# TensorE's order within a slot: the two score tiles ahead of the second transposed chunk, and where the values' products stand

## The reference

```python
x = x + attn_a(layernorm(x), Wq, bq, Wk, bk, Wv, bv, Wo, bo)   # causal mask
x = x + ffn(layernorm(x), g_info, W_qkv, W_proj, b_proj)       # tokens in two classes; a token sees its class and 5 registers
x = x + attn_b(layernorm(x), Wqkv, Wo)                         # rotary embedding, full attention
x = x + ffn(layernorm(x), g_info, W_qkv, W_proj, b_proj)

scores = einsum('bhqd,bhkd->bhqk', Qh, Kh) / sqrt(16)
attn = softmax(scores + mask)
out = einsum('bhqk,bhkd->bhqd', attn, Vh) @ Wo + bo
```

## Time and profile before

| | |
|---|---|
| median of 3 runs | 5044.56 us (5038.67 to 5048.72) |
| the profiled execution | 5051.34 us, span 5049.7 us |
| PE busy | 4459.8 us, 88% of the span |
| DVE, ACT, POOL busy | 64%, 50%, 33% |
| mean granted TensorE clock | 0.965 of full speed |
| stage 0, causal: first to last slot | 1344.4 us, PE busy 1186.9, clock 0.97 |
| stage 1, split | 1337.1 us, PE busy 1166.2, clock 0.94 |
| stage 2, rotary | 1246.5 us, PE busy 1124.9, clock 0.98 |
| stage 3, split | 986.2 us, PE busy 936.7, clock 0.99 |

### The profile page before, as it was taken

One profiled execution on the slowest core, in us unless ns is written; L12 is line 12 of the kernel. 1 busy time (PEld: TensorE's weight loads), 2 busy tenths in 40 slices (PEclk: granted clock), 3 DMA queues, 4 the chain that ended last, 5 costly groups with the idle time before them and its releaser, 6 DMA issues. The chain is left out here.

```text
span 5049.7 us, 70670 instructions
## 1 busy us (share of the span) xinstructions
PE 4459.8 (88%) x26116; PEld 1880.7 (37%) x26116; DVE 3220.1 (64%) x6578; ACT 2547.4 (50%) x3362; POOL 1655.6 (33%) x922
## 2 busy tenths in 40 slices
PE   4899999999869988999886899999999589999999
PEld 2454545455413333333332233333333223333333
DVE  4555555455447677777772766776676277777776
ACT  1444444444425555555453465556555356656555
POOL 2354554545422425344355033333333400000000
PEclk8999999999979999999998899999999889999999
DMA  5353544444323243342432342343344223333331
GB/s 152 99 153 125 148 129 145 133 132 139 97 69 102 83 112 97 94 119 87 113 93 77 83 117 93 105 122 105 95 120 118 66 71 86 86 86 91 89 91 42
DMA packets 302269, 525.23 MB, mean 104 GB/s; under 512 B 58340, under 2 KB 236136, under 8 KB 285544
## 3 DMA queue, kind: packets, MB, share of 16 engines
q1 hardware_dynamic: 259432, 485.06, 33.5%
q10 hardware_dynamic: 42496, 35.66, 2.2%
HBM read 316.97 MB, written 201.46 MB: 103 GB/s over the span
## 5 line engine op out<-in xcount | busy, mean ns | idle before, releaser
L887 DVE TENSOR_REDUCE neg_max<-scores 128x1 f32<-128x512 f32 (+3 forms) x4096 | 2486.6, 636 | 1279.1 <-PE scores L1246 746.4
L1105 ACT ACTIVATE probs<-scores_t 128x1024 f32<-128x1024 f32 (+2 forms) x2048 | 1925.7, 946 | 1571.0 <-PE scores_t L1279 1091.1
L1246 PE MATMUL scores<-k_stack,q_stack 98*128 98x512 bf16 (+4 forms) x4096 | 1435.5, 373 | 285.1 <-DVE neg_max L887 197.8
L1279 PE MATMUL scores_t<-q_stack,k_stack 100*128 100x512 bf16 (+3 forms) x4096 | 1189.3, 364 | 67.7 <-DMA q_stack<-shift_rows 66.4
L1246 PEld LDWEIGHTS scores<-k_stack,q_stack 96*128 96x128 bf16 (+1 forms) x4096 | 397.1, 97 | 1688.0 <-DVE neg_max L887 1240.2
L1300 PE MATMUL o_ps<-probs,values 128*32 128x512 f32 (+1 forms) x8192 | 1019.7, 570 | 0.3 <-ACT probs L1105 0.3
L1279 PEld LDWEIGHTS scores_t<-q_stack,k_stack 100*128 100x128 bf16 x4096 | 377.9, 99 | 389.3 <-issue 142.3
L730 POOL TENSOR_TENSOR parts<-qk_f,parts 128x1024 bf16<-128x1024 f32 x128 | 272.5, 2129 | 678.6 <-ACT parts L1148 519.5
L750 POOL TENSOR_TENSOR sim_inv<-sim_parts,minus_half 128x64 f32<-128x64 f32 x32 | 337.6, 10550 | 206.0 <-DVE sim_parts L970 206.0
L743 POOL TENSOR_TENSOR x_res<-x_res,o_bias_s 128x1024 f32<-128x1024 f32 x32 | 75.5, 2359 | 987.5 <-DMA x_res<-x_after 987.5
L701 POOL TENSOR_SCALAR var_eps<-mean_var 128x4 f32<-128x4 f32 x64 | 14.6, 229 | 1084.5 <-DVE mean_var L851 1084.5
(11 more groups left out here) (118 smaller groups left out, 4045.4 us busy)
## 6 DMA issues: line engine op xcount, KB each, us to landing
q_stack<-q_parts SPq DMA_DIRECT2D x1536, 64.0 KB, 2.7
values<-v_stage SPq DMA_DIRECT2D x64, 1024.0 KB, 4.2
values<-values SPq DMA_DIRECT2D x64, 1024.0 KB, 6.2
k_parts<-parts SPq DMA_DIRECT2D x192, 256.0 KB, 2.7
q_parts<-parts SPq DMA_DIRECT2D x192, 256.0 KB, 4.3
k_stack<-k_parts SPq DMA_DIRECT2D x256, 192.0 KB, 3.2
k_stack<-k_parts SPq DMA_DIRECT2D x256, 128.0 KB, 3.2
x_after<-x_res ACTq DMA_DIRECT2D x48, 512.0 KB, 2.9
```

The costliest lines, as they stand in the source:

```text
L887: nc.vector.tensor_reduce(neg_max[:, h % G, t:t + 1], bank[:, 0:n], AX.X, ALU.max, negate=True).then_inc(max_done.sem, 1)
L1105: nc.scalar.activation(probs[c][:, h % G, 0:n], st[i][:, 0:n], ACT.Exp).then_inc(exp_done.sem, 1)
L1246: last = nc.tensor.matmul(bank[:, 0:n], q[0:r, h, t * P:(t + 1) * P], k[0:r, h, 0:n], start=True, stop=kind != CAUSAL)
L1279: last = nc.tensor.matmul(st[i][:, off:off + L - q0], k[0:ROWS, h, kt * P:(kt + 1) * P], q[0:ROWS, h, q0:L], start=True, stop=kind != CAUSAL)
```

## The change

On PE, m0 and m1 move behind chunk 1, and the values' products move up in front of m2. A slot is now: chunk 0, turns of place 0, chunk 1, m0, m1, values' products, m2, (the extra tile of a split stage's slot 1), m3, turns of place 1. On DVE the list follows: all four maxima stand in the slot's second half, behind whatever belongs to place 0. The semaphores' counts, the tables of turns, buffers, ACT's, POOL's and SP's lists are as before.

```diff
@@ vector block, body @@
                     for place in range(2):
-                        if m:
-                            maximum(B + m[0], m[1], 2 * place)
+                        if place and m:
+                            for t in range(T - 1):
+                                maximum(B + m[0], m[1], t)
                         if place and kind == SPLIT and slot == EXTRA_AT:
                             extra_max(B)
-                        if m:
-                            maximum(B + m[0], m[1], 2 * place + 1)
+                        if place and m:
+                            maximum(B + m[0], m[1], 3)
@@ tensor block, body @@
                     scores_t(B, h0, c, 0)
+                    turns(0)
+                    scores_t(B, h1, c, 1)
                     max_tile(0)
                     max_tile(1)
-                    turns(0)
-                    scores_t(B, h1, c, 1)
+                    if B.n + off >= 0:
+                        output_sums(B + off, g, kt)
                     max_tile(2)
                     if kind == SPLIT and slot == EXTRA_AT:
                         extra_tile(B)
-                    if B.n + off >= 0:
-                        output_sums(B + off, g, kt)
                     max_tile(3)
                     turns(1)
```

## The result

The changed kernel takes 5215.35 us (median of 4 runs, 5210.34 to 5216.99) against 5046.64 us for the kernel before on the same chip: a ratio of 1.0332, 95% interval 1.0312 to 1.0352. It is 3.3% slower; the prediction said 5240 us, 3.9% slower.

A forecast was written before the change was run, and what follows sets the result against it. PE sets the pace, with place-0 turns timed by the turn bank's read and turnless slots by a ring through DVE. Costs of 283 us less gains of 88 give +195, so 5240 us, 3.9% slower; range 5100 to 5340.

The forecast's parts named there:

- item 5: Stage 1's slot 2, behind the long packing of maxima: m3 comes 1.6 us earlier, a gain of 26 us.
- Item 1: Turns of place 0 other than `og`, 21 of 36: m0 and m1 fall onto the path, costing 122 us.
- item 2: `og` turns in place 0 after `sh`, 15 of 36: DVE's shift-row copy comes later too, costing 134 us.
- item 3: In slots at PE's own pace, m3 waits 0.07 us for the maximum of m1, costing 27 us.
- Item 4: Slots without turns stay at 3.11 us against 3.12; only the first behind a turn gains, 19 us in all.
- the ring: In slots without turns, a cycle of waits through DVE times the slot: 3.12 us before, 3.11 after.
- The rival by which a new order saves nothing at two full banks: At the tiles' two banks, a skill's rule on too few PSUM buffers: Item 4 gives 0 instead of 19 us.
- The statistics and the normalisation: Work delaying the maxima of slots 7 to 9: nothing booked, as DVE's list there is as long as before.
- The same: Lost covers and regained waits balance, PE regaining 197.8 us and half of item 2 not coming: 5045 us, chance 0.05.
- Faster: All 192 packings in stages 0 to 2 halt PE, each giving 1.6 us: 4959 us, chance 0.09.
- Much slower: The later shift DMA meets the next batch's loads in two more groups per batch: 128 us more, 5370 us, chance 0.13.
- The check in the waits: In the table of waits, PE's waits for the turn bank, released by ACT and DVE, grow by some 200 us.

The follow-up runs named there:

- the run with that slot alone: Kernel before, with the values' products ahead of m2 in stage 1's slot 2 only: 5030.8 us, ratio 0.9966.
- the split order: Changed kernel with the shift-row copy ahead of m3's maximum and ACT-read turns of place 0 behind chunk 1, DVE-read ones between the chunks: 4948.3 us.
- the fastest version: The split order with one edit: the turn `out` 1 (slot 6), which DVE reads, also behind chunk 1: 4927.9 us, ratio 0.9760.

## Why the prediction was right, point by point

**What bounds the kernel** held: 36 turns per batch of the four stages are timed by the read of the turn bank, and m0 and m1 were its cover. Shown by the idle 0.35 us in slot 6, by that slot coming half-way back for one tile, and, in the three stages that the halt of item 5 does not touch, by 105 of 131 us coming back for other work in the cover's place.

**Item 1 (122 us), item 2 (134 us).** Slot 6 grew by 0.52 us (5.00 to 5.53 in stages 1 to 3), where I had 0.38 and item 3's 0.07; the slots of ACT-read turns 10, 12, 13 in stages 1 and 2 by 0.45 to 0.53, in stage 0 five of nine by 0.28 to 0.33. Item 1's sum held by luck: the slots of its nine turns in stage 0 grew by 1.4 us per batch in all where it booked 3.1 (slot 4 shrank by 0.77), those of the twelve others by 5.8 where it booked 4.6. Slot 4 of stages 1 and 3, whose turn was not on the list, grew by 0.6 us each. The free `og` slots: 0.64 in stage 3 (slots 11 and 15), 0.75 in stages 1 and 2 (slot 11), against my 0.6 to 0.76. In stage 0's slots 7 and 11 only 0.03: there my figure was wrong, as `og`'s wait of 0.63 us took the place of tiles' waits for maxima: these were 1.1 and 0.6 us before and are 0.5 and 0 now.

**Item 4** was right to within 0.08 us: a slot without turns is 3.07 us long in the changed kernel (3.14 before), and 3.52 with only the products moved, which the ring gives. With the slots behind a turn, up to 0.29 us shorter, such slots of stages 1 to 3 without statistics in them gained 1.3 us per batch, 20 us against my 19. The rival by which a new order saves nothing at two full banks, item 4 at 0, did not hold.

**Item 5** was right at its place and incomplete behind it. The timeline of the changed kernel, stage 1, slot 2, answers to the earlier trace rows:

```profile
1983.06 2.37 POOL L743 TENSOR_TENSOR x_res<-x_res,o_bias_s 128x1024 f32<-128x1024 f32 x1
1983.17 2.29 DVE L899 TENSOR_TENSOR shift_parts<-neg_max,shift_parts 128x16 bf16<-128x16 f32 x1
1983.28 1.06 PE L1301 MATMUL o_ps<-probs,values 128*32 128x512 f32 x8
...
1986.24 1.20 PE L1247 MATMUL scores<-k_stack,q_stack 98*128 98x512 bf16 x2 [1.90 <-DVE neg_max L887]
```

The halt is 1.90 us where it was 4.34, and the products run ahead of it at full clock, 1.06 us instead of 1.93. Slot 2 shrank from 9.18 to 6.30 us, 2.88 where I had 1.6; that the halt itself would shorten I had not foreseen. But the lower clock level came all the same, a little later, and lay over slot 3, which grew by 1.56 us:

```profile
1983.00:1986.00 3.00, 1.35 (x10) 0.16 (x8) 2.93 (x3) 1.93 (x3) 2.43 (x2) 0.96 0.68 221
1986.30:1992.50 6.20, 6.20 (x21) 1.89 (x21) 3.86 (x8) 2.05 (x2) 0.00 (x0) 0.50 0.77 187
```

For 6.2 us PE was granted 0.50, its 1.2 GHz level, although it was busy throughout. Net 1.3 us per batch, 21 us against my 26: two errors that nearly cancelled. In the run with that slot alone slot 3 grew as well, and 16 us were left.

**The statistics and the normalisation**, for which I booked nothing: slots 7, 8 and 9 of stage 2 changed by 0.19, 0.54 and -0.88 us, -0.15 in sum.

**The rivals.** *The same* was summed wrongly: by its own conditions the costs are 283 - 67 and the gain 197.8, which leaves 18 us more than before, 5063 us and not 5045. *Faster* would have needed some 140 halts at m2; PE's waits for maxima were 197.8 us in all, and 110.8 are left. *Much slower*: the shift's DMA did decide more in places (stage 0: slot 3 grew by 1.75 us and slot 4 shrank by 0.77; stage 1: slot 15 grew by 1.40), but PE's total wait for it is 62.0 us against 66.4. It moved: in stage 0 the wait ahead of slot 0 fell from 15.3 to 4.6 us and that ahead of slot 4 rose from 4.1 to 15.4.

**The check in the waits** that I named, some 200 us more for the turn bank: 341.8 - 120.4 = 221.4 us. PE's visible waits for maxima fell by 87.0. The two leave 134. The table can't give the whole 166 us, since it shows less than a slot loses: a wait's first part lies under the matmul ahead of it. In the whole span that part, with what the clock took, is PE's 50.0 us more of busy time, and 115.7 are idle.

## What to carry to other kernels

Ask of each piece of work in an in-order list not only what it needs but what it covers: two tiles that nobody waited for were the only thing that PE did while another engine emptied the one bank that its next turn needed. Other work did as well as cover, so when a bank is single, place independent work between its users by the length of the read, and put the read itself ahead of longer work on the reader's list. Look, too, at what the moved piece then stands in front of: `og` right ahead of m0 cost 0.23 to 0.35 us a slot. And a halt that comes from two other engines meeting by chance can go away with any change of order; keep it apart from what the order itself gives.

## What had not been expected of the hardware

The packing's long operations depend on where POOL stands. Before the change, in stage 1's slot 2, where DVE packs the maxima of slot 1:

```profile
2005.49 2.12 POOL L734 TENSOR_TENSOR parts<-rest,parts 128x1024 bf16<-128x1024 f32 x1
2005.54 2.11 DVE L897 CAST shift_parts<-neg_max 128x16 bf16<-128x16 f32 x1
2007.57 2.34 POOL L743 TENSOR_TENSOR x_res<-x_res,o_bias_s 128x1024 f32<-128x1024 f32 x1
```

DVE's second operation on the 16 columns, L899, is the first of the earlier trace rows (2007.68, 2.26). Each of the two ends 0.03 to 0.04 us behind one of POOL's operations (2007.65 and 2007.61; 2009.94 and 2009.91), and takes 2.1 and 2.3 us; without POOL's work it takes 0.17. In the split order the same place looks like this:

```profile
1890.23 2.13 POOL L732 TENSOR_TENSOR rest<-qk_f,parts 128x1024 f32<-128x1024 f32 x1
...
1891.20 1.19 DVE L897 CAST shift_parts<-neg_max 128x16 bf16<-128x16 f32 x1
...
1892.42 0.17 DVE L899 TENSOR_TENSOR shift_parts<-neg_max,shift_parts 128x16 bf16<-128x16 f32 x1
1892.43 2.15 POOL L734 TENSOR_TENSOR parts<-rest,parts 128x1024 bf16<-128x1024 f32 x1
```

The second operation slips in 0.01 us ahead of POOL's next and is short. The Trainium skill, "GPSIMD Engine Reference", in its specifications, says that the two engines share SBUF interfaces and contend where DVE has two SBUF inputs, as L899 has, or runs in a 2-port mode; the trace agrees for L899, and adds the price: up to a whole operation of POOL for each. L897 has one input, and whether it runs in such a mode no run here shows. This chance is worth 4.3 to 5.0 us per batch in stage 1's slot 2 (9.18 us before, 4.15 to 4.85 in eight of the runs), some 75 us, partly taken back in slots 0, 3 and 15. It stands in the sums of all those eight runs, so their totals say less of the order than the stages without it. Of the fastest version's gain, stage 1's slots 2 and 3 alone hold 5.5 us per batch, 87 us of the 119. How much of that is this luck and how much is the order can't be told apart exactly by these runs; no run moved POOL's work against the packing by itself.
